# Graph layer on one core: the first step multiplies adj as it is, and its scales go onto two tiles of G

## What is computed

```python
rowsum = adj.sum(axis=1)                                # adj is 4096 x 4096
d_inv_sqrt = jnp.where(rowsum > 0, rowsum ** (-0.5), 0.0)
normalized_adj = d_inv_sqrt[:, None] * adj * d_inv_sqrt[None, :]
h = jnp.maximum(_layernorm(x, axis=-1), 0.0)            # x is 4096 x 256
out = normalized_adj @ h @ W + b                        # W is 256 x 256
return x + jax.nn.relu(out)
```

## Time and profile before

| what | us |
|---|---|
| median of three runs | 395.7 |
| the three runs | 395.69, 395.70, 397.05 |
| the profiled execution, whole | 396.11 |
| its span in the trace | 394.3 |
| PE busy | 383.9 |
| DVE busy | 319.9 |
| ACT busy | 287.7 |
| POOL busy | 117.2 |
| data moved by DMA, mean rate | 151.87 MB, 385 GB/s |

### The profile page before, as it was taken

One profiled execution on the slowest core, in us unless ns is written; L12 is line 12 of the kernel. 1 busy time (PEld: TensorE's weight loads), 2 busy tenths in 40 slices (PEclk: granted clock), 3 DMA queues, 4 the chain that ended last, 5 costly groups with the idle time before them and its releaser, 6 DMA issues.

```text
span 394.3 us, 5160 instructions
## 1 busy us (share of the span) xinstructions
PE 383.9 (97%) x1750; PEld 318.4 (81%) x1750; DVE 319.9 (81%) x313; ACT 287.7 (73%) x283; POOL 117.2 (30%) x278
## 2 busy tenths in 40 slices
PE   6997999999999999999999999999999999999995
PEld 5885788888888888888888888888888888878884
DVE  4948958978686999959689995868889497899997
ACT  2789989888787778678977869787886777365531
POOL 2450675352121126213224831323323223000000
PEclk9999999999999999999999999999999999999998
DMA  8999999999999999999999999999999986898457
GB/s 283 423 421 418 420 421 421 419 422 423 412 421 421 418 421 421 416 422 421 418 421 421 421 415 422 416 419 423 421 419 412 408 310 218 318 369 325 135 190 262
DMA packets 24217, 151.87 MB, mean 385 GB/s; under 512 B 3328, under 2 KB 3328, under 8 KB 7552
## 3 DMA queue, kind: packets, MB, share of 16 engines
q1 hardware_dynamic: 24192, 151.55, 95.1%
HBM read 147.33 MB, written 4.22 MB: 384 GB/s over the span
## 4 chain that ended last, share of the span: by engine, by line
PE 83%; DMA 8%; DVE 3%; ACT 3%; issue 1%; SPq 1%; POOL 1%; DVEq 0%; ACTq 0%; POOLq 0%
PE moved L840 20%; PE moved L842 19%; PE moved L841 19%; PE held L840 6%; PE held L842 6%; PE held L841 6%; DMA out<-nat 3%; DMA out<-turned 3%; PE held L791 2%; DMA acc<-in_x 1%; DMA turned<-in_x_t 1%; ACT nat L398 1%; DVE lo L652 1%; PE moved L775 1%; PE moved L809 1%; PE moved L811 1%
## 5 line engine op out<-in xcount | busy, mean ns | idle before, releaser
L411 ACT ACTIVATE hi<-at,s 128x1024 fp32r<-128x1024 f32 x112 | 123.0, 1145 | 47.3 <-issue 32.4
L840 PE MATMUL moved<-hi,G 128*128 128x512 f32 x384 | 149.9, 390 | 2.6 <-DVE lo L652 1.2
L652 DVE SCALAR_TENSOR_TENSOR lo<-at,s,hi 128x1024 fp32r<-128x1024 f32 x112 | 141.0, 1278 | 12.5 <-ACT hi L411 12.5
L841 PE MATMUL moved<-lo,G 128*128 128x512 f32 x384 | 149.5, 389 | 0.0
L842 PE MATMUL moved<-hi,G 128*128 128x512 f32 x384 | 149.4, 389 | 0.0
L671 DVE TENSOR_TENSOR acc<-moved,acc 128x1024 f32<-128x1024 f32 x84 | 102.7, 1223 | 50.3 <-PE moved L842 50.0
L398 ACT ACTIVATE nat<-nat 128x2048 f32<-128x2048 f32 x64 | 122.0, 1908 | 6.0 <-DMA nat<-in_adj 5.9
L840 PEld LDWEIGHTS moved<-hi,G 128*128 128x128 f32 x384 | 72.1, 188 | 19.1 <-issue 2.9
L842 PEld LDWEIGHTS moved<-hi,G 128*128 128x128 f32 x384 | 72.1, 188 | 15.0
L841 PEld LDWEIGHTS moved<-lo,G 128*128 128x128 f32 x384 | 72.1, 188 | 14.9
L549 POOL TENSOR_TENSOR row_sum<-part 128x1 f32<-128x1 f32 x32 | 18.0, 562 | 182.5 <-ACT nat L398 182.5
(11 more groups left out here) (69 smaller groups left out, 246.3 us busy)
## 6 DMA issues: line engine op xcount, KB each, us to landing
nat<-in_adj SPq DMA_DIRECT2D x64, 1024.0 KB, 13.2
at<-in_adj_t SPq DMA_DIRECT2D x64, 1024.0 KB, 11.9
acc<-in_x SPq DMA_DIRECT2D x4, 512.0 KB, 7.6
nat<-d_dram SPq DMA_DIRECT2D x2, 1024.0 KB, 5.9
nat<-in_x_t SPq DMA_DIRECT2D x4, 512.0 KB, 4.1
turned<-in_x_t SPq DMA_DIRECT2D x4, 512.0 KB, 4.8
out<-nat SPq DMA_DIRECT2D x4, 512.0 KB, 4.9
turned<-in_x SPq DMA_DIRECT2D x3, 512.0 KB, 14.6
```

The source lines that it names most:

```text
L411: nc.scalar.activation(hi[g % RING][:, 2 * c:2 * c + 2, :], at[g % LA][:, 2 * c:2 * c + 2, :], ACT.Copy, scale=s[:, j:j + 1]).then_inc(hi_ ...
L652: nc.vector.scalar_tensor_tensor(out=lo[g % RING][:, tiles, :], in0=at[g % LA][:, tiles, :], scalar=s[:, j:j + 1], in1=hi[g % RING][:, til ...
L840: nc.tensor.matmul(into[:, f, :], big, hi[g % RING][:, t, :], start=begins, stop=False)
L841: nc.tensor.matmul(into[:, f, :], big, lo[g % RING][:, t, :], start=False, stop=False)
```

## The change

- The first step (slots 0 to 3) takes adj without its scale: `SCALED` is false for step 0, so ACT rounds each of its slots in one piece and DVE makes the rest in one piece, with no wait for s. Instead the two G tiles 0 and 1 get the scale. ACT first copies their product out of PSUM in fp32 into a free part of `acc` (`first_product`), and DVE makes both parts of each tile when its s is there (`make_first_G`).
- In slot 0 PE runs tile 0 for both panels and then tile 1 for both panels, where it ran panel by panel.
- The fourth half row (number 3) is summed by DVE (`sum_last_early`, 128x2048 to 128x1), where ACT summed it. Waits on the count of sums become `wait_summed`.
- `round_slot(1)` moves ahead of both `round_raw` on ACT. DVE makes the statistics of chunk 1 after centring chunk 0.
- The DMA for chunk 1 of x is issued by ACT's queue as its first instruction; SP's queue loses it.
- 16 instead of 14 transpositions of the identity at the start of PE, and 5 more after the first half of chunk 0.
- In `nat_table` g + 4 becomes g + 3: from slot 2 on each half row is loaded and summed one slot later, and `MADE` moves with it.

```diff
+SCALED = [w == 2 and k > 0 for k, w in enumerate(WIDTHS)]
...
-WARM = 14
+WARM = 16
+FILL = 5
...
-        end = min(EARLY + min(2 * (g + 1), g + 4) + max(0, g - 20) // 8, 2 * NB)
+        end = min(EARLY + min(2 * (g + 1), g + 3) + max(0, g - 20) // 8, 2 * NB)
...
+        def first_product(tiles):
+            return acc[:, 0, :, :].rearrange("p f r -> p (f r)").rearrange("p (t f) -> p t f", f=D)[:, tiles, :]
...
+        def wait_summed(eng, m):
+            eng.wait_ge(nat_summed, m + 1 if m < EARLY - 1 else m)
+            if m >= EARLY - 1:
+                eng.wait_ge(last_early_summed, 1)
...
-            load_x(1)
...
             def round_raw(c):
                 act.wait_ge(hW_done, c + 1)
+                product = chunk_product(c)[:, :, :].rearrange("p a (t f) -> p (a t) f", f=D)
+                n = WIDTHS[0] if c == 0 else 0
+                if c == 0:
+                    nc.scalar.copy(first_product(slice(0, n)), product[:, 0:n, :]).then_inc(first_kept, 1)
+                nc.scalar.copy(G[:, BW * c + n:BW * (c + 1), 0, :], product[:, n:BW, :]).then_inc(raw_hi_made, 1)
...
+            act.dma_start(h(1), x[1]).then_inc(x_landed[1], DMA)
...
-            sum_nat(EARLY - 1)
             round_slot(0)
+            round_slot(1)
             round_raw(AHEAD - 2)
-            round_slot(1)
             round_raw(AHEAD - 1)
...
+            def sum_last_early():
+                m = EARLY - 1
+                dve.wait_ge(nat_landed[m % LN], DMA)
+                nc.vector.reduce_sum(part[:, m // 2, m % 2:m % 2 + 1], nat[m % LN][:, :],
+                                     axis=mybir.AxisListType.X).then_inc(last_early_summed, 1)
...
+            def make_first_G(j):
+                own = first_product(j)
+                dve.wait_ge(first_kept, 1)
+                dve.wait_ge(s_ready, j + 1)
+                nc.vector.tensor_scalar(G[:, j, 0, :], own, s[:, j:j + 1], None, ALU.mult).then_inc(first_hi_made, 1)
+                dve.wait_ge(first_hi_made, j + 1)
+                nc.vector.scalar_tensor_tensor(out=G[:, j, 1, :], in0=own, scalar=s[:, j:j + 1],
+                                               in1=G[:, j, 0, :].bitcast(F32), op0=ALU.mult,
+                                               op1=ALU.subtract).then_inc(first_ready, 1)
...
-            for c in range(2):
-                subtract(0, c)
+            make_first_G(0)
+            subtract(0)
+            make_first_G(1)
+            subtract(1)
             rest_of_raw(AHEAD - 2)
-            for c in range(2):
-                subtract(1, c)
             for g, (k, q, panels) in enumerate(SLOTS):
-                if NARROW[k] and NARROW[SLOTS[g + 2][0]]:
+                if NARROW[k] and SCALED[SLOTS[g + 2][0]]:
                     for p in range(2):
                         gather(k, 2 * q + p)
                         subtract(g + 2, p)
+                elif k == 0:
+                    gather(k, 2 * q)
+                    subtract(g + 2)
+                    gather(k, 2 * q + 1)
...
                     if f == 0 and pos == 0:
-                        if j < RAW * BW:
+                        if k == 0:
+                            pe.wait_ge(first_ready, j + 1)
+                        elif j < RAW * BW:
...
+            for _ in range(FILL):
+                nc.tensor.transpose(moved[1][:, 0, 0:P], ident[:, :], ident[:, :])
...
+                if g == 0:
+                    for c in range(WIDTHS[k]):
+                        for p, i in enumerate(panels):
+                            multiply(k, p, i, g, p, c)
+                    continue
```

43 lines of the change are left out of this document (24 added, 19 removed).

## The result

The changed kernel takes **398.46 us** (median of 11 runs, 397.54 to 401.27) against 396.87 for the kernel before (11 runs in the same session); the ratio is 1.0052, 95% interval 1.0037 to 1.0068. The ratios of this document follow the means of the runs (here 398.60 and 396.59) more closely than their medians, which lie only 1.6 us apart. By the ratio the change is slower by 2.1 us, just past the 0.5% that the forecast took as its limit for "slower", with that limit inside the interval. One remark is needed on the base: over all sessions 116 of the 119 runs of the kernel before lie in two groups, 395.3 to 396.5 and 396.6 to 397.7, and two of its three first runs, from which the forecast started, were in the lower one.

The account below looks back on a forecast made before the run. PE bounds the middle; waits bound the front, DVE's and SP's chains the end. Front -0.8 and end +2.7 sum to +1.9; put on the median of 395.7, 397.6 us, own range 396.7 to 398.6, full range 395.2 to 398.9.

Parts of the forecast that it names:

- The sum: Whole kernel: front -0.8 plus end +2.7, with middle and second queue at 0, gives +1.9 us.
- The end: After slot 56: G tile 31 one slot later delays x and slot loads; +2.7 us, bounds 1.65 and 3.9.
- The front: Up to slot 3: waits for s go, PE starts slot 0 at 29.3, waits 2.0 in slot 1; gain 0.8 us.
- slot 2's landing passes one for one to slot 3: Front: if slot 2's load lands 0.5 us later, slot 3 on PE starts that much later.
- the second queue taken at 0: Start: chunk 1 of x on ACT's queue; same bytes pass before slot 2, so 0 us, bounds -1.5 and +0.5.
- the clock is at its full level before them: PE's start: five and two further transpositions stand where PE waits, with the clock already at full level.
- The middle: Between front and end: half rows one slot later cost 0 us, bounds 0 and +1.5.
- Hidden end: End costs 0: 394.9 us with front gain 0.8 (chance 0.08), 392.4 with 3.3 (chance 0.05).
- A higher early rate by the second queue: Front: slot 2 lands 1 us earlier and the front gives 1.8: 396.6 us, chance 0.12.
- Wait for G tile 1: Slot 0: PE waits as before, for this tile instead of s; front 0, 398.4 us; chance 0.25 with the slower rival.
- The slower rival: Panel 0's store lands at 372, or slot 2 0.5 us later; 398.6 us; chance 0.25 together with no front gain.
- The signs of being wrong: Profile after: b added to the last panel of x before 388, or slot 3 starting outside 47 to 49.2.

Follow-up runs that it names:

- e4: The changed kernel with the DMA of chunk 1 of x back on SP's queue behind W: 397.74 us, ratio 1.0026.
- e8: The changed kernel with slot 2's load moved ahead of half rows 4 and 5, right behind slot 1: 399.01 us, ratio 1.0062.
- e13: The changed kernel with 22 instead of 16 transpositions of the identity at PE's start: 398.16 us, ratio 1.0033.
- e3: The kernel before with only the later table of half rows (g + 3 for g + 4): 398.66 us, ratio 1.0049.
- e15: The changed kernel once more, unaltered, run beside e13: 399.64 us, ratio 1.007 to the kernel before.
- e5: The changed kernel with g + 4 back in the table and chunk 1 of x back on SP's queue: 395.41 us, ratio 0.9972.
- e1: The changed kernel with only g + 4 put back in the table of half rows: 396.25 us, ratio 0.9983.
- e9: The changed kernel with g + 4, chunk 1 of x on SP's queue and slot 2's load ahead of half rows 4 and 5: 394.89 us, ratio 0.9963.
- e10: The kernel before with chunk 1 of x on ACT's queue and 22 instead of 14 transpositions at PE's start: 396.81 us, ratio 1.0007.
- e7: The kernel before with only the DMA of chunk 1 of x moved to ACT's queue as its first instruction: 399.25 us, ratio 1.0067.
- e14: The kernel before with only the added transpositions, 16 at the start and 5 after chunk 0's first half: 396.03 us, ratio 0.9987.
- e12: e9's kernel with only the third and fourth load of x waiting for G tile 31, behind slot 60's load: 395.03 us, ratio 0.9962.

## Why the prediction was right or wrong

Ratios to the kernel before, with the queue of chunk 1 set against the rest of the change (us in brackets: ratio less one, times 396.8; each is uncertain by 0.5 to 0.8 us):

| | chunk 1 on SP's queue | on ACT's queue |
|---|---|---|
| kernel before | 1 | 1.0067 (+2.7) |
| new front and added transpositions, g + 4 | 0.9972 (-1.1) | 0.9983 (-0.7) |
| the same, g + 3 (right: the change) | 1.0026 (+1.0) | 1.0052 (+2.1) |

- **The sum, +1.9**, against +2.1 measured: near, but partly by luck, since the measured runs hold executions at half pace, for which the sum has no term. On which side of the limit it falls hangs on a hair, and the forecast's more likely side was the wrong one. The lower ends of its two ranges, 396.7 and 395.2, do not follow from its bounds, which give 396.55 (end 1.65) and 395.05 (second queue -1.5 as well); nothing hangs on it here. The chance of 0.50 was given to "within 0.5%", 0.45 to "slower"; the measured ratio stands at 1.0052, with the limit inside its interval. The predicted 397.6 us was built on a median of 395.7, of mostly lower-group runs; on the base of the comparison it would have read 398.8.
- **The end, +2.7**: the mechanism right in each step, and the size too. The six profiled executions with g + 3 and the old order of SP's loads have 50.3 (e4), 50.9 (e8), 51.0 (e13), 51.1 (e3), 51.5 (the change) and 51.5 us (e15) from slot 56 to the end, so +2.0 to +3.2 against 48.3; by ratios it is +1.9 (e3), +2.1 (e4 less e5) and +2.7 (the change less e1). Loads of x issued at 349.38 (350.35 less the front's gain: 349.5), last b at 390.90 (390.6). The store of panel 0 was forecast to land 25.0 us behind the start of slot 56; it landed 24.7 to 25.2 behind it in five of the six and 25.8 in the first profile of the change.
- **The front, -0.8**: -1.0 in the profile, right in sum and wrong in its parts. PE's slot 0 started at 30.64 and not 29.3, and PE's wait in slot 1 was 0.3 us and not 2.0. Both errors have one cause, the 1.5 us by which chunk 0 landed later, and they cancelled because a second chain, slot 2's landing, was waiting just behind. With chunk 1 on SP's queue both numbers come nearer (29.67; 1.3). There slot 2's landing does gate slot 3 (e5 to e9); in the changed kernel it alone does not (e8), against the step "slot 2's landing passes one for one to slot 3". All this is at full pace; at half pace slot 3 starts at 49.5 to 50.2, and the front gives nothing.
- **The step that failed: the second queue taken at 0**, bounds -1.5 and +0.5, together with "the clock is at its full level before them". As to the bytes it was right: at full pace slot 3 starts at 48.08 with the second queue and at 48.17 without, and the late chunk alone costs the kernel before 0.4 us (e10), inside the bound. What the working left out is PE's pace. With chunk 0 heading the chain of the front and 1.5 us late, PE is idle for longer ahead of it, and in five of the seven profiled executions with 14 or 16 transpositions it then works at half pace up to some 12 us (1.2 GHz by the record of e15). That costs 1.5 us of the whole in the changed kernel (e15 less e13, intervals apart) and 2.4 of the 2.7 us in the kernel before (e7 less e10), beyond the bound of 0.5. The whole times of the second queue in the changed kernel, 0.4 us (e5 to e1) and 1.0 us (e4 to the change), have overlapping intervals, and in the later session the same change came out at +2.8 (e15).
- **The added transpositions** were put at nothing. They are worth 0.5 us by the ratio of e14 (0.9987, 0.9976 to 0.9999), about half of what the whole new front gives (1.1). The profiles speak for the pace as their only use: at full pace e14's execution is as long as that of the kernel before.
- **The middle, 0**: right; no hole between slot 3 and slot 56 in the changed kernel. With g + 4 and an early slot 3 there is one: 0.3 us in e5, 0.7 in e9, 1.0 in e12.
- **The rivals.** Hidden end: refuted (e1, e3). A higher early rate by the second queue: the first slice does carry 309 instead of 283 GB/s, but slot 2 gained nothing that reached PE. Wait for G tile 1: none in the rows of PE. The slower rival came nearest. The store of panel 0 landed at 371.8 in the clock of before, near its 372, in the first profile only; and chunk 0 did yield to chunk 1, but slot 2 did not land later for it (ACT rounds it from 33.93, and from 34.28 in e4), so that the rival, too, missed PE's pace.
- **The signs of being wrong** (last b before 388, slot 3 outside 47 to 49.2) did not show in the first profile. In e15, the same kernel at half pace, slot 3 started at 50.23.

What stays open: why the end takes 50.3 to 51.5 us in six executions whose programs are alike there (the store of panel 0 took 10.4 to 11.9 us), how often the changed kernel runs at half pace, since only one execution of each kernel but this one was profiled, and so how much of the 1.0 us between e4 and the changed kernel is the pace.

## What to carry to other kernels

Ask of each transfer that is issued earlier which one it will share the bandwidth with: here the second queue made the second chunk early and the first one late, and the first one heads the chain. Then look at what the engine that waits for it does next: here PE's products ran at half pace behind a longer wait in most executions, and eight transpositions without a use, which bridge the wait, took away up to 2.4 us. When a wait in a DMA queue's program protects only some of the buffers behind it, split it, or one late tile holds up all loads behind it. Where two chains arrive together, neither shows as the bound when the other alone is moved; look for the pair before giving up an edit that "did nothing".
